# Swin block and depthwise convolution on one core: the next strip's scores moved between the halves of the second layer, the map's shared rows moved by DMA

## What is computed

```python
xs   = roll(layer_norm(x), (-3, -3))           # windows of 7x7 tokens, 16x16 windows an image
q, k, v = windows(xs) @ qkv_w + qkv_b          # 3 heads of 32
p    = softmax(q*scale @ k.T + rel_bias + mask)
x    = x + roll(window_reverse((p @ v) @ proj_w + proj_b), (3, 3))
y    = x + gelu(layer_norm(x) @ fc1_w + fc1_b) @ fc2_w + fc2_b      # hidden 384
z    = depthwise3x3(relu(y)) + dw_bias
out  = batch_norm(z @ pw_kernel + pw_bias)
```

## Time and profile before

| | before |
|---|---|
| median of 3 runs | 5493.09 us |
| the profiled execution, its own time | 5488.53 us |
| its span in the trace | 5486.8 us |
| PE busy | 5291.6 us (96%) |
| DVE busy | 5129.3 us (93%) |
| ACT busy | 5060.9 us (92%) |
| POOL busy | 3786.2 us (69%) |
| granted TensorE clock, mean | 0.993 |
| DMA queue of SP | 12.6% of 16 engines |

### The profile page before, as it was taken

The page is one execution under the profiler, slowest core; times in us unless marked ns, Lnnn a source line. Parts: engine busy times, 40 slices in busy tenths (PEclk is TensorE's granted clock), DMA queues, the critical chain, the costliest instruction groups (busy, mean ns, idle before and its releaser), DMA issues.

```text
span 5486.8 us, 203158 instructions
## 1 busy us (share of the span) xinstructions
PE 5291.6 (96%) x81186; PEld 3789.4 (69%) x81186; DVE 5129.3 (93%) x13773; ACT 5060.9 (92%) x11038; POOL 3786.2 (69%) x4105
## 2 busy tenths in 40 slices
PE   5999999999999999999999999999999999999998
PEld 3767767676766676767777676767676767677675
DVE  4999999999999999999999999999999999999998
ACT  4999999999999999999999999999999989999996
POOL 3777767777777677777777677777777767777673
PEclk9999999999999999999999999999999999999998
DMA  1111111111111111111111111111111111111110
GB/s 25 34 36 35 36 36 37 35 36 35 36 35 36 35 36 35 36 35 36 36 35 38 36 36 35 36 35 36 36 36 36 37 34 36 36 35 36 37 36 24
DMA packets 275650, 193.70 MB, mean 35 GB/s; under 512 B 229160, under 2 KB 246041, under 8 KB 274713
## 3 DMA queue, kind: packets, MB, share of 16 engines
q1 hardware_dynamic: 274712, 180.70, 12.6%
HBM read 77.81 MB, written 77.07 MB: 28 GB/s over the span
## 4 chain that ended last, share of the span: by engine, by line
PE 57%; DVE 19%; ACT 12%; issue 6%; POOL 4%; SPq 1%; DVEq 0%; DMA 0%; ACTq 0%; POOLq 0%
PE bank L428 19%; PE bank L446 18%; DVE smax L819 7%; DVE prob L810 7%; PE bank L535 6%; PE bank L346 6%; PE bank L474 4%; ACT probT L635 4%; POOL prob L954 3%; ACT xT L663 3%; ACT o_tile L599 3%; PE bank L442 3%; DVE acc L850 2%; ACT prob L573 1%; POOL prob L963 1%
## 5 line engine op out<-in xcount | busy, mean ns | idle before, releaser
L850 DVE SCALAR_TENSOR_TENSOR acc<-ymap,taps,acc 96x784 f32<-96x784 f32 (+2 forms) x2176 | 2137.3, 987 | 54.9
L969 POOL TENSOR_TENSOR rstd<-var_eps,minus_half 112x7 f32<-112x7 f32 x512 | 1114.0, 2176 | 1266.0 <-DVE var_eps L883 1266.0
L428 PE MATMUL bank<-x1T,w 96*128 96x448 f32 (+1 forms) x3072 | 1148.3, 510 | 19.7 <-issue 10.5
L446 PE MATMUL bank<-hT,w 128*96 128x448 f32 (+1 forms) x3072 | 1097.1, 493 | 0.0
L627 ACT ACTIVATE hT<-bank,bfc 128x448 f32<-128x448 f32 (+1 forms) x1536 | 772.6, 564 | 11.9 <-PE bank L428 11.4
L428 PEld LDWEIGHTS bank<-x1T,w 96*128 96x128 f32 x3072 | 542.8, 190 | 346.6 <-issue 204.3
L954 POOL TENSOR_TENSOR prob<-prob,smax 128x392 f32<-128x392 f32 x768 | 653.6, 851 | 159.2 <-DVE smax L819 147.0
L980 POOL TENSOR_SCALAR xn<-x_in,minus_mean,rstd 112x96 f32<-112x96 f32 x768 | 680.9, 897 | 45.2 <-POOL offset L972 45.1
L446 PEld LDWEIGHTS bank<-hT,w 128*96 128x96 f32 x3072 | 466.3, 163 | 342.4 <-issue 165.4
L963 POOL TENSOR_TENSOR prob<-prob,srec 128x392 f32<-128x392 f32 x768 | 632.2, 852 | 81.7 <-DVE srec L828 81.7
L682 ACT ACTIVATE ymap<-bank,cols 96x128 f32<-96x128 f32 (+6 forms) x1056 | 603.2, 679 | 92.4 <-PE bank L446 92.4
(11 more groups left out here) (100 smaller groups left out, 10286.4 us busy)
## 6 DMA issues: line engine op xcount, KB each, us to landing
out<-o_tile SPq DMA_DIRECT2D x256, 210.0 KB, 2.5
x_in<-in_x SPq DMA_DIRECT2D x256, 168.0 KB, 2.9
x_in<-in_x SPq DMA_DIRECT2D x256, 126.0 KB, 2.9
k<-qk SPq DMA_DIRECT2D x512, 49.0 KB, 1.9
out<-o_tile SPq DMA_DIRECT2D x256, 84.0 KB, 2.5
hT<-in_L_conv_rel_bias SPq DMA_DIRECT2D x49, 0.6 KB
x1T<-in_L_conv_fc_w SPq DMA_DIRECT2D x1, 144.0 KB, 2.6
w<-in_L_conv_fc_w SPq DMA_DIRECT2D x1, 144.0 KB, 2.4
```

The lines of the kernel that those rows point to most:

```text
L428: pe.matmul(bank[(1, 2, 5)[m]][:, 0:n * PT_], w1[:, m * 128:(m + 1) * 128], x1T[:, first * PT_:(first + n) * PT_], start=True, stop=True). ...
L446: mm = pe.matmul(bank[b][0:C, 0:n * PT_], w2[:, m, :], hT[:, m, first * PT_:(first + n) * PT_], start=False, stop=(m == MC - 1))
L850: last = dve.scalar_tensor_tensor(out=dst, in0=src, scalar=taps[:, i:i + 1], in1=dst, op0=ALU.mult, op1=ALU.add)
L969: pool.tensor_tensor(b["rstd"][:], b["var_eps"][:], minus_half[0:PT_], ALU.pow)\
```

## The change

- TensorE: `scores` of strip t+1 is issued at the end of step t, between the two halves of `second_layer`, in place of at the start of step t+1. Half 1 of the second layer goes to bank 5 in place of bank 4; it waits only for `h_ready`. In `queries_keys` the wait on `ymap_ready` of half 1 stands now ahead of the keys, which write bank 5. `turn_x1` comes after `turn_probs`.
- ScalarE: the order of the step is new. Around the map it is now gelus 0, gelus 1, `first_norm`, `into_map` half 0, `load_exp`, `second_norm`, `into_map` half 1, exps 0 and 1, queries, keys, exps 2. The second write of the shared rows is gone.
- SyncE: one DMA a strip, `move_rows`, copies the two shared rows inside `ymap` after half 1 of the map is written. `tap` 0 of VectorE waits for it.
- VectorE: biases and maxima of different groups alternate, `add_bias` 0 and 1 stand at the end of the step before, tap 8 stands between the maxima of the next step, both `values` copies stand together after two `add_up`, `add_x` comes after tap 4 in place of tap 5.
- GpSimd: `divide` stands at the end of the step before; in the endless sequence its order is the same.

The `values` copies were on VectorE before the change too; only their place is new.

```diff
@@ -187,6 +187,7 @@
         parts_done = [sem("parts1_done"), sem("parts2_done")]
         halves_done = [sem("halves1_done"), sem("halves2_done")]
         ln_ready = [sem("ln1_ready"), sem("ln2_ready")]
+        rows_below = [sem(f"rows_below{i}") for i in range(3)]
         tap_done = sem("tap_done")
 
         shifted, p_ready = sem("shifted"), sem("p_ready")
@@ -270,7 +271,17 @@
                     wait(sp, q_ready, nth(t + 1, 2, u))
                     sp.dma_start(k0[b:b + HD, :], qk[a:a + HD, u * HALF:(u + 1) * HALF]).then_inc(k0_moved, 16)
 
+            def move_rows(t):
+                s = t - 2
+                if not has(s):
+                    return
+                wait(sp, ymap_ready, nth(s, 2, 1))
+                last = area_of_strip(s) + (8 if s % NWIN == NWIN - 1 else 7)
+                below = area_below_strip(s)
+                sp.dma_start(ymap[:, below:below + 2, :], ymap[:, last:last + 2, :]).then_inc(rows_below[s % 3], 16)
+
             def step(t, phase):
+                move_rows(t)
                 move_keys(t)
                 store(t, phase)
                 load(t, phase)
@@ -371,10 +382,11 @@
                 if not has(t + 1):
                     return
                 wait(pe, xt_ready, nth(t + 1, 2, 1))
+                wait(pe, ymap_ready, nth(t - 2, 2, 0))
                 for u in range(2):
-                    wait(pe, ymap_ready, nth(t - 2, 2, u))
                     pe.matmul(bank[3 + u][:, 0:HALF], wqk[:, u, :], xT[:, u * HALF:(u + 1) * HALF],
                               start=True, stop=True).then_inc(q_psum, 1)
+                wait(pe, ymap_ready, nth(t - 2, 2, 1))
                 for u in range(2):
                     mm = pe.matmul(bank[5][64 * u:64 * u + 64, 0:HALF], wk12[:], xT[:, u * HALF:(u + 1) * HALF],
                                    start=True, stop=True)
@@ -432,12 +444,12 @@
                 if not has(t - 1):
                     return
                 first, n = ((0, 4), (4, 3))[half]
-                b = (3, 4)[half]
+                b = (3, 5)[half]
                 if half == 0:
                     wait(pe, pt_ready, nth(t, 3, 2))
+                    wait(pe, out_ready, nth(t - 4, 2, 0))
                 else:
-                    wait(pe, o_ready, nth(t, 1, 0))
-                wait(pe, out_ready, nth(t - 4, 2, half))
+                    wait(pe, h_ready, nth(t - 1, 6, 5))
                 for a in range(n):
                     pe.matmul(bank[b][0:C, a * PT_:(a + 1) * PT_], x1[:, (t - 1) % 2, first + a, :], ident[0:PT_, 0:PT_],
                               is_transpose=True, start=(a == 0), stop=False)
@@ -538,22 +550,22 @@
                     mm.then_inc(proj_psum, 1)
 
             def step(t, phase):
-                scores(t)
                 queries_keys(t)
                 values(t, 0)
                 values(t, 1)
                 pointwise(t, phase, 0)
                 pointwise(t, phase, 1)
                 turn_x(t)
-                turn_x1(t)
                 turn_probs(t, 0)
                 turn_probs(t, 1)
                 turn_probs(t, 2)
+                turn_x1(t)
                 weigh_values(t, phase)
                 hidden(t, 0)
                 project(t)
                 hidden(t, 1)
                 second_layer(t, 0)
+                scores(t + 1)
                 second_layer(t, 1)
 
             steps(pe, step)
@@ -674,9 +686,8 @@
                     parts = [(0, 4, area + 2), (4, 3, area + 7)]
                 else:
                     parts = [(0, 7, area + 2)]
-                parts.append((5, 2, area_below_strip(s)))
                 wait(act, y_psum, nth(s, 2, half))
-                src = bank[(3, 4)[half]][0:C, 0:n * PT_].rearrange("p (j r c) -> p j r c", j=n, r=WS)
+                src = bank[(3, 5)[half]][0:C, 0:n * PT_].rearrange("p (j r c) -> p j r c", j=n, r=WS)
                 for r0, nr, row in parts:
                     dst = ymap[:, row:row + nr, 1:1 + HW].rearrange("p r (c j) -> p j r c", j=WS)
                     last = act.activation(dst[:, first:first + n], src[:, :, r0:r0 + nr, :], ACT.Relu,
@@ -702,28 +713,28 @@
                     normalise(1, t, x1n, x1[:, t % 2], x1n_ready)
 
             def step(t, phase):
-                probs_turned(t, 1)
-                probs_turned(t, 2)
-                x1_turned(t)
-                attention_out(t)
-                load_gelu(t)
-                gelus(t, 0)
-                first_norm(t, phase)
-                gelus(t, 1)
-                load_exp(t)
-                into_map(t, 0)
+                second_norm(t)
                 into_map(t, 1)
-                second_norm(t)
-                queries(t + 1)
                 exps(t + 1, 0)
                 exps(t + 1, 1)
+                queries(t + 1)
                 keys(t + 1)
                 exps(t + 1, 2)
                 outputs(t + 1, (phase + 1) % UNROLL, 0)
                 outputs(t + 1, (phase + 1) % UNROLL, 1)
                 x_turned(t + 1, 0)
+                probs_turned(t + 1, 0)
+                probs_turned(t + 1, 1)
                 x_turned(t + 1, 1)
-                probs_turned(t + 1, 0)
+                probs_turned(t + 1, 2)
+                x1_turned(t + 1)
+                attention_out(t + 1)
+                load_gelu(t + 1)
+                gelus(t + 1, 0)
+                gelus(t + 1, 1)
+                first_norm(t + 1, (phase + 1) % UNROLL)
+                into_map(t + 1, 0)
+                load_exp(t + 1)
 
             steps(act, step)
 
@@ -837,6 +848,7 @@
                 low = top + TOP_ROWS + ((c + 1) % NWIN + 1) // NWIN
                 if i == 0:
                     wait(dve, ymap_ready, nth(c + 1, 2, 1))
+                    wait(dve, rows_below[c % 3], 16 * (c // 3 + 1))
                     wait(dve, pw_psum, nth(t - 5, 2, 1))
                 else:
                     wait(dve, tap_done, nth(c, 9, i - 1))
@@ -908,28 +920,28 @@
                 norm_stats(1, t, x1[:, t % 2], LN_EPS)
 
             def step(t, phase):
-                add_bias(t, phase, 0)
                 find_max(t, 0)
-                add_bias(t, phase, 1)
+                add_bias(t, phase, 2)
                 find_max(t, 1)
-                add_bias(t, phase, 2)
+                tap(t - 1, (phase + 3) % UNROLL, 8)
                 find_max(t, 2)
-                values(t, phase, 0)
                 add_up(t, 0)
                 add_up(t, 1)
+                values(t, phase, 0)
+                values(t, phase, 1)
                 add_up(t, 2)
-                values(t, phase, 1)
+                norm_x(t, phase)
                 tap(t, phase, 0)
-                norm_x(t, phase)
                 tap(t, phase, 1)
                 tap(t, phase, 2)
                 tap(t, phase, 3)
                 tap(t, phase, 4)
+                add_x(t, phase)
                 tap(t, phase, 5)
-                add_x(t, phase)
                 tap(t, phase, 6)
                 tap(t, phase, 7)
-                tap(t, phase, 8)
+                add_bias(t + 1, (phase + 1) % UNROLL, 0)
+                add_bias(t + 1, (phase + 1) % UNROLL, 1)
 
             steps(dve, step)
 
@@ -1000,9 +1012,6 @@
                     rest(1, t, x1n, x1[:, t % 2], x1n_rest)
 
             def step(t, phase):
-                divide(t, 0)
-                divide(t, 1)
-                divide(t, 2)
                 first_scale(t)
                 first_rest(t, phase)
                 second_scale(t)
@@ -1010,6 +1019,9 @@
                 shift(t + 1, 0)
                 shift(t + 1, 1)
                 shift(t + 1, 2)
+                divide(t + 1, 0)
+                divide(t + 1, 1)
+                divide(t + 1, 2)
 
             steps(pool, step)
 
```

## The result

| | before | changed |
|---|---|---|
| median of the first 4 runs each | 5496.8 us | 5551.7 us (5540.3 to 5567.0) |
| ratio, 95% interval | | 1.0092 (1.0072 to 1.0111) |
| the same two kernels in a later comparison, 19 and 10 runs | 5500.5 us | 5525.7 us, ratio 1.0043 (1.0022 to 1.0063) |
| span of the profiled execution | 5486.8 us | 5547.5 us |
| period of a strip, median | 20.85 us | 21.05 us |

A forecast was written before the change was run, and what follows sets the result against it. No single engine but closed loops, A and B, were taken to bound the kernel. The keys' wait, +59 us, and image ends, -9, gave 5538.5 us profiled, 5543 as median; range 5470 to 5590.

The forecast's parts named there:

- The new wait: TensorE's keys wait for ScalarE's map half 1, behind table load and second norm: +0.23 us a strip, bounds 0.14 to 0.31.
- Loop A's own work: Same matmuls and same seven ScalarE copies in another order: 0, bound -0.05 us a strip, -12 us.
- Loop B relieved: Scores move earlier, leaving 0.94 us of slack before the output copy; worth nothing in the usual strip, only at image ends.
- loop A: Loop without slack: TensorE from hidden to pointwise's end, ScalarE from second output copy through xT, probT, x1T, back to hidden.
- loop B: Softmax loop: scores, bias 0, maxima, POOL shift, ACT exp 2, output copy; claimed to end within hundredths of loop A.
- Image ends -9 us: Period over an image's end is 0.59 us longer, VectorE being late; some 15 places relieved: -9 us, bounds 0 and -9.
- The shared rows: ScalarE loses two writes a strip, SyncE issues one more DMA: cost 0; without cover 1.9 us a strip.
- The norm's readiness and VectorE: GpSimd's offset ready for second_norm with 1.1 us to spare, add_x coming earlier; VectorE fits, but only just.
- R2: Rival: VectorE becomes the bound, add_x not earlier, second_norm late: +0.90 us a strip, 5714 us; chance 0.09.
- The table load: On ScalarE between map half 0 and second norm: load takes 1.28 us, next instruction 0.01 us after, no drain.
- R3: Rival: the table switch costs a further 1.38 us drain, +1.26 us on ScalarE's path, 5864 us; chance 0.01.
- The sum: 255 strips x 0.23 = +59 us, image ends -9, giving 5538.5 us for the profiled run, 5543 for the median.

The follow-up runs named there:

- e1: Changed kernel with into_map half 1 ahead of second_norm on ScalarE; 5502.1 us, ratio 0.9998 to the kernel before.
- e4: Changed kernel with the shared rows written by ScalarE again and no DMA of rows; 5610.7 us, ratio 1.0190.
- e2: Changed kernel with load_exp ahead of into_map half 0 on ScalarE; 5461.8 us, ratio 0.9917 to the kernel before.
- e9: Kernel before with x turned ahead of pointwise on TensorE and xT copied ahead of the outputs on ScalarE; 5453.2 us, ratio 0.9903.
- e6: e2 plus x turned ahead of pointwise, xT copied ahead of the outputs, queries ahead of exp 1; 5378.0 us, ratio 0.9769.
- e8: e2 plus queries ahead of exp 1 on ScalarE, TensorE's order unchanged; 5448.5 us, ratio 0.9892.
- e5: Kernel before with only the DMA of the two shared rows, ScalarE writing them no longer; 5509.1 us, ratio 1.0009.

## Why the prediction was right, point by point

- **The new wait, right, with some luck in its size.** It was priced at 0.23 us a strip between bounds of 0.14 and 0.31; the period grew by 0.20. The sign and the place were right, and e1 to e4 each move it as the theory says. In parts it is less exact. From the start of second layer half 0 to the keys, the kernel before takes 2718.52 - 2711.43 = 7.09 us and the changed one 2713.30 - 2705.93 = 7.37: +0.28. Within that, TensorE alone would have taken 7.03 (the keys wanted at 2712.96), so the wait is 0.34 us, above the 0.31 that the term allowed, and not 0.23. The period grew by 0.20 because 0.14 us of other work went away at the same time (0.06 here, 0.08 in the next point), which the prediction had at 0. ScalarE's path from the end of half 0 was put at 4.90 us and took 4.95 (2708.35 to 2713.30).
- **Loop A's own work** was put at 0 with a bound of -0.05. It was -0.08: hidden to second layer 5.85 us against 5.90, pointwise to hidden 5.69 against 5.73, keys to pointwise 2.13 against 2.12. I had treated two things as fixed. TensorE's small steps at a change of work come and go with the neighbours (the 0.05 here, and the 0.06 above: half 0 took 2.36 us to the next start and not 2.26, but half 1 2.02 and not 2.08, and the queries 1.42 and not 1.52). And the seven copies from xT to the end of x1T took 3.55 us in the new order (2717.52 to 2721.07) and not 3.59 (2701.89 to 2705.48). Together this is why e2, without the wait, has a period 0.13 us shorter than the kernel before and not an equal one.
- **Loop B relieved:** right in kind, and far too large in size. VectorE waits for scores 11 times. But the slack was put at 0.94 us, and ScalarE had 0.33 left ahead of the output copies:

```profile
2715.67 0.54 ACT L585 ACTIVATE prob<-prob 128x392 f32<-128x392 f32 x1
2716.54 0.93 ACT L611 COPY o_tile<-bank 112x384 f32<-112x384 f32 x2 [0.33 <-PE bank L535]
```

  From bias 0 (2709.69) to the end of exp 2 (2716.21) it took 6.52 us where 5.75 was forecast to the output copy. The prediction left out that the queries' copies now stand between exp 1 and exp 2, and it took GpSimd's shift as unchanged (last section). That the relief alone is worth nothing was not run by itself. e9, with loop A cut and loop B untouched, puts B 0.09 us below A, so that the relief has nothing to win while A stands; it took the removal of the wait (e2) and of loop A (e6) to turn it into time.
- **Image ends -9 us:** right in kind, near 6 us in size. It is hidden slack, and other orders lose it again: an end costs 0.68 us in e1 and 1.10 in e2, over two distances each, 0.56 in e8 and 1.35 in e6. The period alone does not set this, as e1 with 20.95 and e8 with 20.70 show.
- **The shared rows:** 0 by their DMA was right. e5 shows 0 in the kernel before, and no wait for the rows or the keys' copy appears. But the change needs them: without the DMA its loss would be 0.61 us a strip (e4).
- **The norm's readiness and VectorE:** right. Offset ends and add_x begins nearly as the steps said, seen in POOL's and DVE's rows of the changed kernel:

```profile
2708.99 0.78 POOL L984 TENSOR_TENSOR offset<-minus_mean,rstd 112x7 f32<-112x7 f32 x1
```

```profile
2703.51 0.95 DVE L917 TENSOR_TENSOR x<-bank,x_in 112x384 f32<-112x384 f32 x2
...
2709.69 1.04 DVE L821 TENSOR_TENSOR prob<-bank,table 128x392 f32<-128x392 f32 x2
```

  The offset is there at 2709.77, 1.19 us before the norm starts (1.1 was forecast). The biases start at 2709.69, 0.10 us after scores end (2709.59), so VectorE fits with hundredths, as forecast. The sign named for this step, add_x waiting for the projection, is there, though small:

```profile
DVE x L917 <- PE bank L547: 66.2, 100, 5.1
```

  VectorE took 14.86 us from the biases to add_x (2709.69 to 2703.51 + 21.04) and not 14.38, so it came there with about 0.2 us to spare and not 0.5, by my estimate. R2 did not occur.
- **The table load:** the changed kernel shows again 1.28 us and the next instruction 0.01 us after it. R3's further drain, which the Trainium skill (ScalarE: Activation LUTs, What ACT_TABLE_LOAD costs) states, is not in any trace of this case. By the rate that the same section of the Trainium skill gives for an ACTIVATE, an estimate, both maps together would take 0.73 us less than the rows of before said, more than the wait of 0.34. The changed kernel's own rows, 1.09 and 0.85 us, decided.
- **The sum.** +59 - 9 = +50 us was forecast. The first comparison gave +55 (5551.7 - 5496.8), the second +25, the period +50; that the second lies at half of the forecast is the chance part. The chance part, stretches at the lower clock, had no term in the sum and is as large as half of the effect.

What I did not see at all is how cheap the remedy was. The prediction says that ScalarE is idle ahead of map half 0, and prices the load behind it, without drawing the conclusion that the load belongs into that idle time.

## What to carry to other kernels

When three engines are all above 90% busy, find the closed loop before pricing anything: the rows where one engine starts 0.05 us after another ends, in every period. Work taken off an engine is worth its full time on the loop (0.41 us in e4) and nothing off it (0 in e5). If a reordering moves a buffer's writer later, price the path to its release on the other engine against what the first does meanwhile, and put fixed work such as a table load into the idle time ahead of the wait rather than behind it. Compare periods beside medians where stretches at a lower clock make the medians wander by half a per cent.

## What I had not expected of the hardware

The clock of single strips. In the profile of the changed kernel five strips ran at a mean granted clock of 0.76 to 0.81 of full speed, a mixture of its two levels of 1.2 and 2.4 GHz, between stretches at 1.00, and each cost 6 to 9 us. Their number, 0 to 5 in eleven profiles, follows no edit that I made. But they do not come out of an even stream. PE at one of them, and a stretch shortly behind, with a granted clock of 0.50 where it was 1.00 before the stop:

```profile
2332.17 0.59 PE L486 MATMUL bank<-probT,vw 49*32 49x49 f32 x39 [0.29 <-ACT probT L647]
2334.03 0.29 PE L486 MATMUL bank<-probT,vw 49*32 49x49 f32 x9 [1.27 <-issue]
2334.25 4.85 PE L440 MATMUL bank<-x1T,w 96*128 96x448 f32 x6
```

```profile
2337.00:2341.00 4.00, 4.00 (x15) 2.75 (x14) 0.30 (x1) 2.11 (x5) 0.00 (x0) 0.50 0.00 0
```

TensorE stops for 1.27 us in the middle of the attention matmuls, waiting for nothing that the profile shows ("issue"), and the six hidden matmuls behind the stop take 4.85 us in place of 2.52. All 20 such strips of the eleven profiles have a stop of this kind, of 0.66 to 2.6 us, within 2 us of the fall. The stop is not enough by itself: five more of 0.95 to 1.27 us in the changed kernel's trace brought no such strip. What stops TensorE, and why only some stops bring the lower clock, stays open.

GpSimd's instructions changed their length with their neighbours. The group of `shift` in the changed kernel's page, and in that of the kernel before (busy us, mean ns | idle before):

```profile
L966 POOL TENSOR_TENSOR prob<-prob,smax 128x392 f32<-128x392 f32 x768 | 819.9, 1080 | 84.2 <-DVE smax L830 41.2
```

```profile
L954 POOL TENSOR_TENSOR prob<-prob,smax 128x392 f32<-128x392 f32 x768 | 653.6, 851 | 159.2 <-DVE smax L819 147.0
```

The same work on the same tile takes 1080 ns in place of 851, now that it runs beside other VectorE instructions (a tap among them). At most it used up slack of loop B, since ScalarE still sat idle 0.33 us ahead of the output copies. In a kernel closed through GpSimd it would be 0.7 us a strip, by an estimate from three groups of 0.23 us. Why it slows was not tested.
